# Sums of squares in a grouped norm: one full-precision product with ones before the last output chunk, or two rounded products after it

## The reference, cut to what matters

```python
yg = y.reshape(B, L, G, GROUP_SIZE)                   # 8 groups of 512
var = jnp.mean(yg * yg, axis=-1, keepdims=True)
yn = (yg * lax.rsqrt(var + EPS)).reshape(B, L, I) * norm_weight
yn = yn * jax.nn.silu(gate)
out = jnp.einsum('bli,di->bld', yn, out_proj_w)
```

## Time and profile before

| | before |
|---|---|
| median of 3 runs | 3430.32 us (3430.1 to 3430.79) |
| profiled execution: its time | 3429.23 us |
| profiled execution: its span | 3427.5 us |
| TensorE busy | 3396.0 us (99%) |
| VectorE busy | 3030.7 us (88%) |
| ScalarE busy | 1403.5 us (41%) |
| GpSimd busy | 447.6 us (13%) |
| mean granted TensorE clock | 0.995 |

### The profile page before, as it was taken

The page is one execution under the profiler, slowest core; times in us unless marked ns, Lnnn a source line. Parts: engine busy times, 40 slices in busy tenths (PEclk is TensorE's granted clock), DMA queues, the critical chain, the costliest instruction groups (busy, mean ns, idle before and its releaser), DMA issues. The chain is left out here.

```text
span 3427.5 us, 58336 instructions
## 1 busy us (share of the span) xinstructions
PE 3396.0 (99%) x19725; PEld 2871.4 (84%) x19725; DVE 3030.7 (88%) x4814; ACT 1403.5 (41%) x2168; POOL 447.6 (13%) x326
## 2 busy tenths in 40 slices
PE   7999999999999999999999999999999999999999
PEld 5788888888888888888888888888888888888888
DVE  6899999999999999999999999999999999998443
ACT  5555544444344443444443444434444344433111
POOL 1201110011110111101111011110111101111333
PEclk8999999999999999999999999999999999999999
DMA  6432363334533353334433363335423352224331
GB/s 239 184 127 105 122 216 128 128 110 167 176 116 122 113 206 135 116 122 170 149 135 118 121 207 112 135 123 180 149 105 135 126 181 98 76 95 153 93 92 59
DMA packets 207793, 466.23 MB, mean 136 GB/s; under 512 B 35152, under 2 KB 80624, under 8 KB 198286
## 3 DMA queue, kind: packets, MB, share of 16 engines
q1 hardware_dynamic: 206784, 464.78, 38.3%
q0 software_dynamic: 304, 0.82, 0.1%
q10 hardware_dynamic: 672, 0.24, 0.0%
HBM read 313.69 MB, written 152.09 MB: 136 GB/s over the span
## 5 line engine op out<-in xcount | busy, mean ns | idle before, releaser
L995 PE MATMUL p_cv<-ht,wt 128*128 128x512 f32 x5376 | 1274.5, 392 | 2.3 <-DVE xc L1219 2.2
L995 PEld LDWEIGHTS p_cv<-ht,wt 128*128 128x128 f32 x5376 | 1004.0, 188 | 225.9 <-issue 11.1
L1087 PE MATMUL bank<-wot,gy 128*128 128x512 f32 x3072 | 728.2, 392 | 0.0
L1087 PEld LDWEIGHTS bank<-wot,gy 128*128 128x128 f32 x3072 | 572.0, 188 | 120.9
L1128 ACT ACTIVATE xc<-p_cv,cvb,cvw 128x512 f32<-128x512 f32 x256 | 200.0, 782 | 904.7 <-PE p_cv L995 904.5
L1219 DVE SCALAR_TENSOR_TENSOR xc<-p_cv,cvw,xc 128x496 f32<-128x496 f32 (+2 forms) x768 | 545.1, 717 | 22.5
L995 PE MATMUL bank<-ht,wt 128*128 128x512 f32 x2304 | 554.5, 389 | 0.0
L995 PEld LDWEIGHTS bank<-ht,wt 128*128 128x128 f32 x2304 | 431.9, 188 | 89.2
L982 POOL TENSOR_TENSOR r<-rv,neg_half 128x4 f32<-128x4 f32 x64 | 89.9, 1405 | 2367.6 <-DVE rv L1299 2367.6
L1237 DVE TENSOR_TENSOR m<-cbm,y 128x1024 f32<-128x1024 f32 x256 | 295.9, 1217 | 0.0
L979 POOL TENSOR_TENSOR segr<-adts,mask_le 128x1024 fp32r<-128x1024 f32 x128 | 243.0, 1919 | 336.1 <-DVE adts L1202 335.9
(11 more groups left out here) (190 smaller groups left out, 3419.3 us busy)
## 6 DMA issues: line engine op xcount, KB each, us to landing
ht<-h_d SPq DMA_DIRECT2D x63, 2048.0 KB, 7.8
acc_d<-acc SPq DMA_DIRECT2D x64, 1024.0 KB, 4.3
wt_d<-wnext SPq DMA_DIRECT2D x112, 512.0 KB, 3.1
acc<-acc_d SPq DMA_DIRECT2D x56, 1024.0 KB, 7.0
wt<-wt_d SPq DMA_DIRECT2D x70, 512.0 KB, 8.6
stage<-in_L_attn_in_proj_w SPq DMA_DIRECT2D x85, 256.0 KB, 2.7
wot<-wt_d SPq DMA_DIRECT2D x28, 512.0 KB, 7.0
xb<-in_x SPq DMA_DIRECT2D x8, 1024.0 KB, 8.3
```

The lines of the kernel that those rows point to most:

```text
L995: ins = pe.matmul(pb[:, :], wt[:, n, l, k, :], ht[:, rr, k, :], start=(q == 0 and k == 0), stop=(q == 2 and k == KC - 1))
L1087: ins = pe.matmul(bank[OUT[t]][:, :], gy[:, c, l, t * P:(t + 1) * P], wot[:, rr, c, :], start=(c == 0 and q == 0), stop=(c == CT - 1 and q ...
```

## The change

The sum of the squares, `y` chunk 0, is split into a high part (ScalarE, a copy into a rounded tile) and a low part (VectorE, a subtraction) in a new tile `ysum`, which lies over chunks 1 and 2 of `y`. TensorE multiplies both parts by a rounded column of ones, adding them in PSUM: eight rounded products instead of four plain ones. They stand behind the last chunk of the output projection instead of ahead of it, so at the border to the next pass. On VectorE two `join` operations move from behind `rv` to ahead of it. One memset of the rounded ones is added at the start.

```diff
+    ysum = nc.alloc_sbuf_tensor_at("ysum", [P, 2, BLK], F32R, offset=RAW_AT + 4 * (NCV + CT + 1) * BLK)
...
+    ones_r = sh.ones_r = sb("ones_r", [P, NSQ], F32R)
...
             for c in range(CT):
-                if c == CT - 1:
-                    pe.wait_ge(s_y, CT * it + CT + 3)
-                    pe.wait_ge(s_sqsum, (CT - 1) * (it + 1))
-                    for t in range(TT):
-                        ins = pe.matmul(bank[SSQ][:, t * NSQ:(t + 1) * NSQ], y[:, 0, t * P:(t + 1) * P], sh.ones[:, 0:NSQ],
-                                        start=True, stop=True)
-                    ins.then_inc(s_ssq, 1)
                 pe.wait_ge(s_ulo, CT * it + c + 1)
...
+            pe.wait_ge(s_y, CT * it + CT + 3)
+            pe.wait_ge(s_sumlo, it + 1)
+            for t in range(TT):
+                for half in range(2):
+                    ins = pe.matmul(bank[SSQ][:, t * NSQ:(t + 1) * NSQ], ysum[:, half, t * P:(t + 1) * P], ones_r[:, :],
+                                    start=(half == 0), stop=(half == 1))
+            ins.then_inc(s_ssq, 1)
...
             high(2)
             high(3)
+            act.wait_ge(s_sqsum, (CT - 1) * (it + 1))
+            act.activation(ysum[:, 0, :], y[:, 0, :], ACT.Copy).then_inc(s_sumhi, 1)
...
             pair(5, ld, 7)
+            dve.wait_ge(s_sumhi, it + 1)
+            dve.tensor_tensor(ysum[:, 1, :], y[:, 0, :], ysum[:, 0, :].bitcast(F32), ALU.subtract).then_inc(s_sumlo, 1)
             join(2, la, lc)
             join(1, lb, ld, 9)
             pair(6, lc, 10)
             pair(7, ld, 11)
+            join(1, lc, ld, 13)
+            join(2, lb, lc, 14)
             dve.wait_ge(s_ssq, it + 1)
-            w8_step(13)
+            w8_step(15)
             dve.tensor_scalar(rv[:, :], bank[SSQ][:, 0:TT * NSQ].rearrange("p (t n) -> p t n", t=TT)[:, :, 0], 1.0 / GI, EPS,
                               ALU.mult, ALU.add).then_inc(s_rv, 1)
-            join(1, lc, ld)
-            join(2, lb, lc, 14)
-            join(3, la, lb, 15)
+            join(3, la, lb)
             w8_step(16)
```

More of the change, by code:

```diff
@@ L352, in gpsimd_part @@
         pool.memset(byte_ones[:, :], 1).then_inc(s_const, 1)
+        pool.memset(sh.ones_r[:, :].bitcast(F32), 1.0).then_inc(s_const, 1)
     def tensor_part(pe):
@@ L831, in attend_part @@
     s_ssq = sem("s2_ssq")
+    s_sumhi = sem("s2_square_sum_high")
+    s_sumlo = sem("s2_square_sum_low")
     s_rv = sem("s2_rv")
```

## The result

| | before | changed |
|---|---|---|
| median, us | 3430.01 (3428.45 to 3434.26, 20 runs) | **3435.57** (3433.55 to 3437.46, 20 runs) |
| ratio to before | | 1.0016, 95% interval 1.0010 to 1.0022 |
| profiled execution, us | 3429.23 | 3434.32 |
| its span, us | 3427.5 | 3432.6 |

The change costs 5.6 us, 0.16%. That lies within the 0.2% that the forecast called "same", and 3435.57 lies in its range of 3427.0 to 3442.0; its own figure was 3432.6, a loss of 2.3. The forecast's mechanism in the loop holds. Most of the loss comes from a place that it gave one short sentence, the border of the stages.

What follows compares the result with a forecast made beforehand. The prediction took TensorE's instructions in a row to bound the loop. To the profiled 3429.23 us, 1.1 below the median 3430.32, it added +0.4, +1.1, +0.4, -0.2 and +0.6 (total +2.3 on the median): 3432.6 us, range 3427.0 to 3442.0.

Steps and rivals of the forecast that it cites:

- What bounds the kernel: In a mid-loop pass of 47.48 us TensorE is busy throughout, VectorE 44.47; the loop costs TensorE's instructions in a row.
- TensorE's own work: Sum-of-squares products in each pass: eight rounded ones cost 0 to 0.05 us less than four plain ones; -0.03 taken.
- VectorE's way: VectorE's chain to the next pass: subtraction adds 0.61 us, copy and `rv` waits are covered, `acc` starts 0.86 later (0.67 to 0.94).
- What TensorE can bear: Cover at `project(3)` before a late `acc` stalls TensorE: 0.86 us in passes 16 to 55, less in the first 16.
- The sum of the loop: Loop terms: 40 passes +0.4 us, 15 passes +1.1, pass 9 +0.4, last eight passes -0.2.
- The end: Border of the two stages after the last pass: follows the last `acc`, 0.86 us later; +0.6 us taken.
- the first (VectorE's delay beyond its cover): Rival in the loop: late `acc` stalls `project(3)`, 5.6 us per further 0.1 us of delay, 3441 us; 15%.
- the loop's branch: Rival at the loop's end: short products leave the branch less time, 0.2 us per pass, 3443 us; 5%.
- Rounded products: Rival on TensorE: rounded products much cheaper, half of 0.92 us per pass; 3401 us, or 3429 if VectorE limits; 3%.
- Nothing moves: Rival: wake-up behind `r` 0.05 us, no stalls, products 0.03 cheaper, 3429 us; 25 of the forecast's 77%.
- The signs: Expected in the changed profile: `rv` 0.5 us behind the next pass's first matmul, POOL releasing `acc`, near-zero `project(3)` distance, 47.5 us passes.
- The bound for being wrong: In the loop: TensorE idle 0.1 us or more, released by the convolution, would show the forecast wrong.

## Why the prediction was right in the loop and wrong at the end

- *What bounds the kernel*: right. TensorE is busy in the whole of each pass, and VectorE's one hand-over at `project(3)` decides about stalls. The pair of kernels with one more operation shows the cover of 0.6 and more before, and none after.
- *TensorE's own work*, -0.03 taken, bounds 0 and -0.05: outside its bounds, -0.087. The eight products cost what they cost before, and so does the first distance behind them, 0.315 at the old place and 0.319 at the new. What the forecast missed lies behind that: over passes 57 to 61, the twenty distances that follow at the old place, up to the tenth matmul of the next pass, average 0.231 instead of 0.227, which makes 0.09 in all. They come in two runs of nine, one behind the products and one from the first matmul of the next pass. The forecast took the 24 matmuls there for undisturbed, 0.229 apart, but nine of their distances are slow and the others are 0.227. With the products at the border the matmuls behind them keep 0.227, plain or rounded; with the products two tiles earlier one such run, of eight, is left. Why the place matters stays open.
- *VectorE's way*: right to the hundredth. The subtraction takes 0.60 from start to start (0.61 forecast), ScalarE's copy is covered (from the last addition of squares to the operation behind the two `pair`s it is 1.52 us, 1.53 before), `rv` is 2.38 later, counted from the start of `dtx` (2.37), the wake-up behind `r` is 0.22, and `acc` is 0.87 later against 0.86. The low part was ready at 1681.85 for products that ran at 1684.29.
- *What TensorE can bear*: nearly right. Of the margin of 0.79, the kernel before with one more operation has 0.18 left after 0.61, as it should. In the changed kernel `acc` is 0.87 late and TensorE 0.087 early, so the load of `project(3)` falls 0.87 + 0.09 - 0.79 + 0.05 = 0.22 behind its place in the stream, and a stalled pass pays 0.14 for it. So the lead of a load over its matmul forgives 0.08, not the 0.12 that the forecast added. Two kernels with a longer delay give the same 0.08: with one more operation `acc` is 1.48 late, the load 0.83 behind, and a pass pays 0.76; with the joins back it is 1.93, 1.28 and 1.20. In the trace the distance from the waiting matmul to the next is 0.337 instead of 0.227 (passes 16 to 54), and the nine after it lose another 0.03.
- *The sum of the loop*: +0.4, +1.1, +0.4, -0.2 is +1.7, and 1.36 was measured, but not in these shares, so that the sum is near is in part luck. Passes 16 to 56 lose 0.057 each, +2.3 (forecast +0.4); passes 0 to 8 and 10 to 15 together gain 0.4 (+1.1); pass 9 loses 0.06 (+0.4); the last seven gain 0.6 (-0.2). That passes 0 to 8 would share in TensorE's gain had not been seen, and the stall, which the forecast put into the early passes, lies in the later ones.
- *The end*, "`acc` is 0.86 later; I take +0.6": **this is the step that failed**, a term of the sum that was mis-sized: +4.0 measured. It looked at `acc` alone. But GpSimd's queue holds two memsets behind the last `r`, and TensorE waits for them; `rv` stands behind the last products now, which end at 3150.26, and `r` ends at 3152.03, 1.8 us later. Before, the second memset ended at 3148.57, 0.45 ahead of the first convolution product; now it ends at 3152.15, and that product starts 2.28 later than it would (3103.62 + 46.50 = 3150.12). The remaining 1.70 is the clock. The run with early memsets shows both gone, and `acc` as late as ever without a cost.
- *The rivals*: the first (VectorE's delay beyond its cover) is what the loop does, at 0.05 net per pass and so within the forecast's own band. No gap appeared at the loop's branch: from the first of the eight products to the next work it is 0.80 us there, 0.81 at the old place. Rounded products were not cheaper at all. "Nothing moves" was wrong.

The signs came as foretold: `rv` behind the first matmul (0.73, 0.5 foretold), `acc` released by POOL, and the distance at `project(3)` near zero. The pass of 47.5 held as well. The bound for being wrong, TensorE idle for 0.1 us or more behind the convolution, was passed: the weight loads idle 0.29 there, and the pass is 0.14 longer by it.

## What to carry to other kernels

When a result moves later, go through every instruction that is queued behind its consumers, on each engine and past the end of the loop: two memsets of 0.12 us in a queue that "has nothing else to do" cost more here (4.0 us) than all that the change did to 64 passes (1.36 net). A move that looks free in the steady pass has to be costed once more in its last iteration, where no next pass covers it; and the wait of 2.1 us on TensorE brought 1.7 us more of slower products, 2.9 in one profile. When a change bundles a new form of an operation with a new place for it, run the place alone: here it held all of the gain, and the new form of the products none: what the split added was work on VectorE, and that cost 7.5 us.

## What was not expected of the hardware

- Around a wait of 2.1 us or more, TensorE's clock fell to 1.2 GHz: for the 3.4 us from 3153.2 to 3156.6 in the changed kernel, and for 3.4 to 6.9 us at the same place in all seven profiles of kernels with the products at the border and the memsets behind `r`. In the five others, where it waits there for 0.24 us or not at all, no such stretch stands there.
- GpSimd's subtraction of 128x512 took 2.56 us beside VectorE, where VectorE's own takes 0.68. In 62 of 64 passes a VectorE integer operation that began under it took 1.5 us instead of 0.54, while the two `join`s under it took their usual time.
- Behind the eight 2-column products, and the one longer distance that follows them, the next twenty distances of matmuls of 512 columns average 0.231 us where the products stand ahead of the last chunk, and 0.227 where they stand behind it.
